# A chunked delta-rule attention with a routed expert layer: four corners of TensorE for every 64x64 product, and a new order of the chunk

## What is computed

```python
xn = layernorm(x) * ln_w + ln_b
q, k, v = xn @ Wq.T, xn @ Wk.T, xn @ Wv.T          # 16 heads of 64
alpha, aR = sigmoid(xn @ Wa.T + ba), sigmoid(xn @ WaR.T + baR)
beta, gamma = sigmoid(xn @ Wb.T + bb), sigmoid(xn @ Wg.T + bg)
def step(S, R):                                     # for each position
    kn = k_t / max(norm(k_t), 1e-12)
    r = clip(v_t - S.T @ kn, -1, 1)
    S = a_t[:, None] * S
    S = S + b_t * outer(kn, v_t - S.T @ kn)
    R = aR_t[:, None] * R
    R = R + g_t * outer(kn, r - R.T @ kn)
    o = S.T @ q_t + R.T @ q_t
x = x + layernorm(o @ Wo.T + residual)              # then the experts, on layernorm(x)
```

## Time and profile before

| | us |
|---|---|
| median of three runs | 3297.05 |
| the profiled execution, its own time | 3276.76 |
| its span | 3274.9 |
| TensorE matmuls busy (share of the span) | 2773.5 (85%) |
| VectorE busy | 2721.3 (83%) |
| ScalarE busy | 1943.8 (59%) |
| GpSimd busy | 953.5 (29%) |
| mean granted clock of TensorE | 0.906 |

### The profile page before, as it was taken

The page is one execution under the profiler, slowest core; times in us unless marked ns, Lnnn a source line. Parts: engine busy times, 40 slices in busy tenths (PEclk is TensorE's granted clock), DMA queues, the critical chain, the costliest instruction groups (busy, mean ns, idle before and its releaser), DMA issues. The chain is left out here.

```text
span 3274.9 us, 132532 instructions
## 1 busy us (share of the span) xinstructions
PE 2773.5 (85%) x55642; PEld 2460.6 (75%) x55642; DVE 2721.3 (83%) x6827; ACT 1943.8 (59%) x5180; POOL 953.5 (29%) x928
## 2 busy tenths in 40 slices
PE   3888888888888888888888888888886199999986
PEld 3878888887787888788788888888786177777664
DVE  2889898888989988999999999999997156777776
ACT  2656555556666655666666555666654077666664
POOL 3112222222222222223222222233221101444444
PEclk8988898888888988989999899999998599999998
DMA  3321111111111111111111111111110945777776
GB/s 116 82 64 37 36 35 35 35 35 37 39 35 35 37 37 35 43 35 35 39 40 41 35 35 35 35 42 35 39 40 30 347 144 170 221 217 224 220 217 180
DMA packets 209563, 264.55 MB, mean 81 GB/s; under 512 B 30673, under 2 KB 183250, under 8 KB 208210
## 3 DMA queue, kind: packets, MB, share of 16 engines
q1 hardware_dynamic: 183936, 188.53, 19.0%
q0 software_dynamic: 24576, 67.27, 7.2%
q10 hardware_dynamic: 466, 0.27, 0.0%
HBM read 125.37 MB, written 130.58 MB: 78 GB/s over the span
## 5 line engine op out<-in xcount | busy, mean ns | idle before, releaser
L379 POOL DMA_INDIRECT table<-tail,places x256 | 277.1, 1082 | 721.1 <-DVE BR L852 214.8
L1496 PE MATMUL bank<-w,tail 128*128 x1280 | 357.2, 401 | 31.4 <-ACT tail L1539 14.5
L1468 POOL DMA_INDIRECT tail<-y_table,places x256 | 249.5, 975 | 449.3 <-DMA y_table<-tail 314.0
L1091 POOL COPY inv_r<-N 32x512 f32<-32x512 f32 x128 | 136.4, 1065 | 734.0 <-DVE N L827 730.0
L445 DVE TENSOR_TENSOR tri<-tri,step 128x58 f32<-128x58 f32 (+13 forms) x896 | 305.5, 341 | 30.8
L444 DVE TENSOR_TENSOR step<-tri 128x58 f32<-128x58 f32 (+13 forms) x896 | 301.4, 336 | 26.4
L1496 PEld LDWEIGHTS bank<-w,tail 128*128 128x128 f32 x1280 | 219.2, 191 | 95.9 <-issue 72.7
L1586 DVE TENSOR_TENSOR more<-tail 128x1 f32<-128x1 f32 x320 | 50.8, 159 | 193.7 <-ACT tail L1548 189.6
L1511 PE MATMUL bank<-w,tail 128*128 x640 | 191.1, 380 | 2.7 <-DVE tail L1597 1.4
L1546 ACT ACTIVATE tail<-bank 128x129 f32<-128x129 f32 x320 | 89.8, 281 | 158.9 <-PE bank L1496 156.3
L1482 PE MATMUL bank<-ident,tail 128*128 128x128 f32 x640 | 125.1, 278 | 66.1 <-DMA tail<-table 65.6
(11 more groups left out here) (275 smaller groups left out, 8103.8 us busy)
## 6 DMA issues: line engine op xcount, KB each, us to landing
table<-blank SPq DMA_DIRECT2D x320, 128.5 KB, 3.2
tail<-table SPq DMA_DIRECT2D x320, 128.5 KB
y_table<-tail SPq DMA_DIRECT2D x320, 128.0 KB
w<-in_wpack_dram SPq DMA_DIRECT2D x16, 1540.0 KB, 19.3
tail<-in_x_dram SPq DMA_DIRECT2D x66, 64.0 KB, 2.5
x_rows<-tail SPq DMA_DIRECT2D x32, 128.0 KB
sh_rows<-tail SPq DMA_DIRECT2D x32, 128.0 KB, 1.9
table<-tail,places POOLq DMA_INDIRECT x256, 2.9
```

Source lines behind the costliest of these rows:

```text
L379: nc.gpsimd.indirect_dma_start(out=table, out_offset=bass.IndirectOffsetOnAxis(ap=t.places[:, TOP * (n - 1) + k:TOP * (n - 1) + k + 1], ax ...
L1468: nc.gpsimd.indirect_dma_start(out=t.term[2 * (m % 2) + k], out_offset=None, in_=d.y_table[0:P * closed(b) + P + 1, :], in_offset=bass.Ind ...
L1496: mm = nc.tensor.matmul(ps[:, 0:257], t.xT_slot[i % 3][:, P * kt:P * kt + P], weights(i, 257 * kt, 257), start=(kt == 0), stop=(kt == 1))
```

## The change

All small products now go through `four`, with the units split between two banks as `pair`, `mixed` or `out_unit` say; tiles that are written in one split and read in another are addressed through `at_pair` and `at_mixed`. The state terms of O and PR stand ahead of the inverses, half of each with `flip`, and their banks are held till they are done. X1 stands behind PR. The key norms are made right after k and q, in a tile of their own (`norms`). The adds to S stand ahead of the keys. Half the triangles stand behind W, the others behind O's last term, and RU follows. ScalarE makes xnT for the next turn ahead of the decay of R, and empties X1 behind the decays. `Order` now hands a bank to the next user from a queue, to which banks of O and PR return at the marks ("free", ...). The cut diff:

```diff
     jobs = [("XT", "")] * front + two("KS") + two("a") * front + two("KR") + two("r") * front + [("BG", "")] * front
     jobs += [("RT", "")] + [("PQ", str(i)) for i in range(4)] + two("k") * front + [("RL", "")] + two("RQ")
-    jobs += [("KT", f"{g}{h}") for g in range(2) for h in range(2)] + two("q") * front + [("SG", "")]
-    jobs += two("Z") + two("X") + two("PR") + two("U") + two("SU") + two("NS") * front + two("O") + [("SD", "")]
-    jobs += two("W") + two("RU") + ends + [("RK", "")] * route + [("OUT", "")] + two("V") * front
+    jobs += [("KT", f"{g}{h}") for g in range(2) for h in range(2)] + two("q") * front + two("NS") * front + [("SG", "")]
+    jobs += two("O") + two("PR") + two("Z") + [("X", "0")] + two("U") + free("PR") + [("X", "1")] + two("SU")
+    jobs += [("SD", "")] + two("W") + ends[0:2] + free("O") + ends[2:4] + two("RU")
+    jobs += [("RK", "")] * route + [("OUT", "")] + two("V") * front
...
+def odd(i, s):
+    return 2 * i + s
+
+
+def pair(i, s):
+    return 4 * (i // 2) + 2 * s + i % 2
+
+
+def mixed(i, s):
+    return 2 * i + (s ^ i % 2)
+
+
+def out_unit(i, s):
+    b1 = i // 2 % 2
+    return 8 * (i // 4) + 4 * (s ^ b1) + 2 * b1 + i % 2
...
+            def four(banks, unit, pairs, first=True, last=True, whole=False, rows=range(8), flip=0):
+
+                for i in rows:
...
                             for j in range(2):
-                                r, to = slice(C * j, C * j + C), slice(C * (j ^ s), C * (j ^ s) + C)
+                                r, to = slice(C * j, C * j + C), slice(C * (j ^ s ^ flip), C * (j ^ s ^ flip) + C)
                                 mm = nc.tensor.matmul(banks[s][to, C * i:C * i + C], lhsT(r, u), rhs(r, u),
...
+            def crossed(n, name, unit, pairs):
+                for ins in four(both(n, name), unit, pairs):
                     ins.then_inc(t.sem["mm_done"], 1)
...
-            def products(ps, h, pairs):
-
-                for i, u in enumerate(range(8 * h, 8 * h + 8)):
-                    for m, (lhsT, rhs) in enumerate(pairs):
-                        for j in range(2):
-                            r = slice(C * j, C * j + C)
-                            mm = nc.tensor.matmul(ps[r, C * i:C * i + C], lhsT(r, u), rhs(r, u),
-                                                  start=(m == 0), stop=(m == len(pairs) - 1))
...
+                for e in range(2):
...
+                        for h in range(2):
+                            u = pair(4 * e + m, h)
+                            for j in range(2):
+                                r, to = slice(C * j, C * j + C), slice(C * (j ^ h), C * (j ^ h) + C)
+                                mm = nc.tensor.matmul(banks[h][to, 2 * C * m:2 * C * m + 2 * C], t.kminus[0][r, u, :],
+                                                      t.pq[r, :, u, :], start=True, stop=True)
...
-                for h in range(2):
-                    units(n, f"RQ{h}", h, [(of(t.kminus[1]), of(t.rqplus))])
+                crossed(n, "RQ", pair, [(of(t.kminus[1]), of(t.rqplus))])
...
-                    for h in range(2):
-                        units(n, f"KT{g}{h}", h, [(of(t.kminus[g]), lambda r, u: t.eye[r, :])])
+                    crossed(n, f"KT{g}", pair, [(of(t.kminus[g]), lambda r, u: t.eye[r, :])])
...
                         projection(n, f"q{i}", t.wq, i)
+                    pe.wait_ge(t.sem["keys_squared"], n + 1)
+                    for i in range(2):
+                        ps = begin(n, f"NS{i}")
+                        norm_matmul(nc, t, ps, i).then_inc(t.sem["front_mm"], 1)
...
+
+                O, PR = both(n, "O"), both(n, "PR")
+                queries = [(of(t.S), lambda r, u: t.pq[r, 1, u, :]), (of(t.R), of(t.rqplus))]
+                keys = [(lambda r, u: t.pq[r, 0, u, :], of(t.S))]
+                four(O, out_unit, queries, last=False, whole=True, rows=(2, 3, 6, 7), flip=1)[1].then_inc(t.sem["O_flipped"], 1)
+                four(PR, mixed, keys, last=False, whole=True, rows=(1, 3, 5, 7), flip=1)[1].then_inc(t.sem["PR_flipped"], 1)
+                pe.wait_ge(t.sem["O_flipped"], n + 1)
+                four(O, out_unit, queries, first=False, last=False, whole=True, rows=(0, 1, 4, 5))
+                pe.wait_ge(t.sem["PR_flipped"], n + 1)
+                four(PR, mixed, keys, first=False, last=False, whole=True, rows=(0, 2, 4, 6))[1].then_inc(t.sem["O_begun"], 1)
...
-                for g in range(2):
-                    wait_emptied(pe, t, o, n, f"Z{g}")
-                    ps = begin(n, f"X{g}")
-                    for u in range(16):
...
-                PR = [begin(n, "PR0"), begin(n, "PR1")]
-                four(PR, odd_unit, [(lambda r, u: t.pq[r, 0, u, :], of(t.S))], last=False, whole=True)
+                second_product(0)
...
                 pe.wait_ge(t.sem["inv_s_ready"], n + 1)
-                crossed(n, "U", [(of(t.inv[0]), of(t.B))])
+                crossed(n, "U", mixed, [(of(t.inv[0]), of(t.B))])
                 wait_emptied(pe, t, o, n, "U1")
-                for ins in four(PR, odd_unit, [(lambda r, u: t.pqT[r, u, 0, :], of(t.U))], first=False, whole=True):
+                for ins in four(PR, mixed, [(of_pq(0), of(t.U, at_mixed))], first=False, whole=True):
                     ins.then_inc(t.sem["PR_done"], 1)
...
-                for h in range(2):
-                    units(n, f"SU{h}", h, [(of(t.kT[0]), of(t.U))])
-                if front:
...
-                O = [begin(n, "O0"), begin(n, "O1")]
-                ins = four(O, pair_unit, [(of(t.S), lambda r, u: t.pq[r, 1, u, :]), (of(t.R), of(t.rqplus)),
-                                          (of(t.U), lambda r, u: t.pqT[r, u, 1, :])], last=False, whole=True)
-                ins[1].then_inc(t.sem["O_begun"], 1)
...
+                second_product(1)
+                crossed(n, "SU", pair, [(of(t.kT[0], at_pair), of(t.U, at_mixed))])
+                four(O, out_unit, [(of(t.U, at_mixed), of_pq(1))], first=False, last=False, whole=True)
...
                 pe.wait_ge(t.sem["BR_ready"], 2 * n + 2)
-                crossed(n, "W", [(of(t.inv[1]), of(t.BR))])
+                crossed(n, "W", mixed, [(of(t.inv[1]), of(t.BR))])
+                if front:
+                    triangles(n, [0])
                 wait_emptied(pe, t, o, n, "W1")
-                for ins in four(O, pair_unit, [(of(t.B), of(t.rqT))], first=False, whole=True):
+                for ins in four(O, out_unit, [(of(t.B, at_mixed), of(t.rqT, at_pair))], first=False, whole=True):
                     ins.then_inc(t.sem["O_done"], 1)
-                for h in range(2):
-                    units(n, f"RU{h}", h, [(of(t.kT[1]), of(t.B))])
-                if front:
-                    triangles(n)
+                if front:
+                    triangles(n, [1])
+                crossed(n, "RU", pair, [(of(t.kT[1], at_pair), of(t.B, at_mixed))])
...
                     route_weights(nc, t, link, t.xrow[n % 2])
+                dve.wait_ge(t.sem["O_begun"], n + 1)
+                for h in range(2):
+                    ps = mm(n, f"SU{h}")
+                    nc.vector.tensor_tensor(by_pair(t.S, h), in_pairs(ps), by_pair(t.S, h),
+                                            ALU.add).then_inc(t.sem["dve_emptied"], 1)
...
-                    link(nc.vector.tensor_tensor(keys, keys, t.tri[:].rearrange("p c i -> p (c i)"), ALU.mult))
+                    link(nc.vector.tensor_tensor(keys, keys, t.norms[:], ALU.mult))
...
-                dve.wait_ge(t.sem["O_begun"], n + 1)
-                for h in range(2):
-                    ps = mm(n, f"SU{h}")
-                    nc.vector.tensor_tensor(t.S[:, half[h], :], blk(ps[:, :]), t.S[:, half[h], :],
-                                            ALU.add).then_inc(t.sem["dve_emptied"], 1)
...
                     nc.vector.tensor_copy(t.dec_end[(n + 1) % 2][:], t.dec[:, :, :, C - 1]).then_inc(t.sem["queries_made"], 1)
+                if front:
+                    masked(n)
                 for h in range(2):
...
-                if front:
-                    masked(n)
...
+            def next_inputs(n):
+                ps = mm(n, "XT")
+                for kt in range(2):
+                    ins = nc.scalar.activation(t.xnT[:, kt, :], ps[:, P * kt:P * kt + P], ACT.Identity,
+                                               bias=t.lnb[:, kt:kt + 1], scale=t.lnw[:, kt:kt + 1])
+                ins.then_inc(t.sem["front_act"], 1)
+
...
             diagonal(-1, 1)
+            next_inputs(0)
...
                 ln_guess(2, norms + 1)
-                if front:
-                    ps = mm(n, "XT")
-                    for kt in range(2):
-                        ins = nc.scalar.activation(t.xnT[:, kt, :], ps[:, P * kt:P * kt + P], ACT.Identity,
-                                                   bias=t.lnb[:, kt:kt + 1], scale=t.lnw[:, kt:kt + 1])
-                    ins.then_inc(t.sem["front_act"], 1)
...
                     front_copy(n, "k1", t.k[:, half[1], :])
```

(29 more changed lines are left out.)

149 lines of the change are left out of this document (79 added, 70 removed).

## The result

The changed kernel takes **3373.38 us** (median of 4 runs, 3354.57 to 3383.45) against 3299.00 (3291.89 to 3310.26) of the kernel before in the same comparison: ratio 1.0216, 95% interval 1.0156 to 1.0275. It is 74 us slower. The prediction said 3265, with 3195 to 3320 as its range: wrong in sign and outside the range. The rival "Half clock at r for twice as long" came nearest in its time (3341).

A forecast was written before the change was run, and what follows sets the result against it. VectorE's own work was taken as the bound: 73.74 + 0.1 (RU) + 1.85 (L755) + 0.9 (clock) = 76.6 us a chunk against 77.12. That gave 3257, then 3265 us after giving back half the median's excess; range 3195 to 3320.

The forecast's parts named there:

- Half clock at r for twice as long: Slower rival, 17%: 6.8 us of half clock makes r, BG and PQ slow; 79.0 us a chunk, 3341 us.
- The wait for the norms goes: Norms in mid-chunk on ScalarE remove VectorE's wait at L859, 43.1 us in all, with nothing late next there.
- Four corners: TensorE's small products speed up: RQ from 2.08 to 1.16 us, PQ from 3.71 to an assumed 1.9.
- The new wait: VectorE waits 1.85 us a chunk at L755 for ScalarE's guess, now queued behind xnT and R's decay.
- D + 1.5: Predicted end of XT on TensorE, 1.5 us after VectorE opens the next chunk with the transpose at L778.
- the wait for E: RU starts only once VectorE empties the banks of A00 and A01; half clock over the first triangles hides there.
- The clock: TensorE idles 4.2 us before r, so r runs at half clock; this and smaller clock losses cost 0.9 a chunk.
- the third rival: The slower-side case, 17%: half clock lasts over r, BG and PQ, with 2.3 us of waiting at L809; 3341 us.
- State terms first, X1 behind PR: Ahead of U, TensorE loses half of X and a PR product: PR 2.0 us earlier, inverses in time by 0.6.
- TensorE late: Rival, 18%: PQ keeps 3.71 us or the clock stays low; U 1.2 us later or more, 3289 to 3304 us.
- S added ahead of the keys: On VectorE, two adds move ahead of plus_made: nothing in VectorE's sum, and the triangles start at 1542.2.
- triangles behind W: On TensorE, half the triangles follow W and RU comes last; the 0.31 us wait at the triangles goes.

The follow-up runs named there:

- the best kernel: Changed kernel with xnT behind the guess, O's state terms behind SU, S adds behind the keys, all triangles behind O's last term: 3205.21 us, ratio 0.9717.

## Why the prediction was wrong, point by point

**The sum, term by term.** Forecast: 73.74 + 0.1 + 1.85 + 0.9 = 76.6. Measured: own work and small gaps 79.39 - 6.45 = 72.94; R and the triangles 0.38 for 0.1; L801 2.50 for 1.85; PQ 1.36 for 0.4; PR 2.21 for 0.3 and the tail's 0.2. PQ and PR together are 3.57 for 0.9, 2.7 of the 2.8 by which the chunk was missed; the others nearly cancel. One sum is off by 2 us: 3257 and the 10 given back for the median make 3267, and not 3265.

**The wait for the norms goes: right.** Nothing of the earlier trace rows's 43.1 is left.

**Four corners: right.** RQ's 64 records take 1.16 (2.08 before), PQ's 1.98 (3.71), for which I had taken 1.9. The rule of the Trainium skill ("TensorE: Matmul & The Clock Gate", What overlaps and what doesn't), weighed in the prediction, would have had RQ and PQ gain nothing. The trace speaks against it: both orders go from one row group to the other at each product, only the columns are new, and the time is nearly halved.

**"The new wait": right in kind, 2.50 for 1.85.** XT ended at 1500.87, D + 2.5 and not D + 1.5. At the end of the chunk shown it is the same: RU starts at 1569.68, XT ends at 1579.23, and the next D is 1576.72. From RU's start XT took 9.55 for my 9.17, since RU took 1.48 for 1.03, and D came after 7.04 for my 7.65, since VectorE's own work behind RU was shorter than I had it (the last section shows where). The slow first triangle (1.77) and O's term (1.95), after 3.9 us of waiting for kplus, did hide behind the wait for E, as I had said: VectorE doesn't wait for the triangles there.

**"The clock": the term that was mis-sized at r.** Half clock came over r as forecast (0.54 over 3.44 us, r in 5.33 for 3.84), and in chunks like the one shown it cost about the 0.6 that I had worked out. But I took it to end with r. In 15 chunks of 31 it went on over PQ, with waits of 1.5 to 2.9 us, which is what the third rival said. The run with the pause filled shows that all 1.36 of PQ's wait came of the pause. The Trainium skill's rule that pauses between bursts cost the clock (same page, Why this matters for your kernels) stood in the prediction as a warning; the trace agrees with it at both new pauses, 3.85 us ahead of r (5.33 for 3.84) and 3.86 ahead of the first triangle (1.77 for 1.16).

**"State terms first, X1 behind PR": the step that failed.** It said that U waits only for ScalarE's X0, that TensorE is in time at the inverses by 0.6, and PR 2.0 us earlier. In the chunk shown N ends at 1538.05 and TensorE starts at 1538.69, 0.6 late (0.7 on average), which I had priced as the rival "TensorE late". What I had not seen at all is the 1.75 us inside Z, and that ScalarE's second inverse diagonal (1.24) stands behind the copies of Z and ahead of the copy of X0, so that a late Z makes X0 late. Then U and PR run at half clock, since TensorE waited 2.88 ahead of them: 2.18 and 1.99 for 1.56 and the 1.16 of a four-corner product. PR is ready later after N than before, and VectorE waits 2.21 a chunk for it. O's state terms are the part that did it: with them behind SU again U starts 6.6 us after N on average, and 6.5 in the best kernel, for 8.9 here, and nearly no pause is left inside Z. They are worth 1.66 a chunk in the best kernel; out of the change they gave 0.72, as the adds to S began to wait. The half clock over U and PR is not what makes PR late: in the best kernel both take 1.9 us as well, and PR is hardly waited for.

**"S added ahead of the keys" and "triangles behind W": I costed both at nothing.** Within the change the adds don't wait. But the two tie up the order: the adds need O's terms begun, the first triangle needs the adds done. With O late the adds wait 2 us a chunk (64.5 / 31). Moving the adds alone loses 0.5%, moving the triangle with them gains 1.1% in all.

**The rivals.** "Half clock at r for twice as long" had the right sign and place for one of its terms (PQ 2.3, measured 1.36), but put 0.8 at PR, where 2.21 lay. The harm was this rival and "TensorE late at the inverses" at once; I had priced each with the other at its best value, and so no case of mine reached 3373.

**Open.** Whether the pause inside Z is a shortage of instructions is argued below, not shown. Half clock over U and PR was not taken away by itself. X1 behind PR and PR's early state term stayed in all the changed kernels, so their worth is not known. The four corners were not undone alone, since every reader of their tiles would change.

## What to carry to other kernels

A transfer or copy that is made "one turn ahead" stands in its engine's order ahead of something else: here xnT, wanted by nobody yet, delayed a short guess by 2.5 us and the clock of the next product with it, and cost 3.8 to 4.7 us a chunk. Parts of a reordering should be tried both out of the change and into the best version: norms in mid-chunk read as a loss (+0.8%) alone and as a gain of 4.9 us a chunk beside the rest. One profiled execution can lie 20 us off its kernel's median and turn the sign of a small difference. And forecast cases that share an engine have to be priced together, not as alternatives.
